# Stringing the first layer's feed-forward and the second layer's normalisation between the value and key tiles of the second layer

## The chip, the cores and the metric

The kernel runs on one core of a Trainium2 chip. The metric is the device time of one execution in microseconds (us), and the median of three runs is given. Smaller is better.

## The reference

A hidden state `x` of 16 x 64 = 1024 tokens by 512 features goes through two transformer layers, each with an attention to a fixed context `ctx` of the same shape and a feed-forward part. Each of the four parts reads a normalised `x` and adds its result to `x`:

```python
x = x + xattn0(layernorm(x), ctx, ctx, mask, Wq, Wk, Wv, Wo)       # 32 heads, 8 KV heads of 128, rope, tanh cap
x = x + lora_moe(layernorm(x), A, B, Wr)                           # 4 experts of rank 16, two chosen by a router
x = x + xattn1(layernorm(x), ctx, Wq, Wk, Wv, Wo)                  # 16 heads, 4 KV heads of 96
x = x + ffn1(layernorm(x), W, bias, A, Bf, coeffs, scales)         # dense 512x512 plus 16 weighted low-rank terms
# lora_moe: logits = x @ Wr.T; gates = softmax over the top 2;  mid = x @ A.T;  out = 4 * sum_e gates[e] * (mid[e] @ B[e].T)
# xattn1: keys and values are taken from concat(ctx, layernorm(x)); queries from layernorm(x)
```

What matters here: the feed-forward of the first layer (`lora_moe`) is small, and it stands as a chain between two attentions. Of the second attention, the keys and values of the context half depend on nothing in that chain; the queries and the keys and values of the other half do.

## The kernel before, in words

**Tiling.** The 1024 tokens are 8 tiles of 128, and the tiles 0 to 3 (`LO`) and 4 to 7 (`HI`) are normalised as two halves. Large products are made of three fp32r products (high by high, high by low, low by high: `thrice`, L1082), so each weight is split in a high part by ScalarE (ACT) and a low part by GpSimd (POOL): a `split` step. PSUM has eight banks `PB`. Banks are dealt out in turn from a list, `ring`, while banks 2 and 3 are at times reserved.

**What sets the order.** `plan()` (L63) writes out by hand one list of named steps. Every engine then walks this same list and issues what it has to do in each step, waiting on semaphores. So the list fixes the order of work on every engine at once: TensorE (PE), VectorE (DVE), ACT, POOL and the DMA queue on SyncE (SP). A blocked instruction holds up everything behind it on its engine.

**The steps that the change moves.**

- `e0(u, c)`: the first attention's output product of token tile c (12 matmuls of 512 columns); DVE adds it to `x`.
- `stats(ph, i)`, `rstd(ph, i0)`: DVE takes mean and variance of tile i, then, for four tiles at once, the reciprocal root in 12 dependent instructions. `ph` is 1 for the normalisation ahead of the feed-forward, 2 for the one ahead of the second attention.
- `xn(ph, i)` (L723): ACT writes the normalised tile into `Eb[i % 2]`; from the third tile on it waits until the tile two before it has been transposed. `xT(ph, i)`: PE transposes it (four transposes).
- `ffn_xT(i)` (L769): ACT copies the transposed tile to `pTb[i % 2]`. `mid(hf, c)`: PE multiplies it with the experts' A and the router (8 matmul instructions of 68 columns).
- `gates(hf)` (L981): on DVE, 13 steps of small dependent instructions for the router's choice of a half (a line of ACT, the exponential, in the middle), then four products that apply the gates. It waits for all four `mid` of its half.
- `mgT(hf)`: PE transposes the gated products, and ACT copies them to SBUF. `delta(i)`: PE multiplies with B (two matmul instructions of 512 columns), and DVE adds the result to `x`.
- `xsplit(2, i)`: ACT takes the high part of the transposed tile from PSUM, DVE the low part, which also frees the bank.
- `v1(w, i)` (12 matmuls of 384 columns; w = 0 is the context half, w = 1 the half from `x`), `k1(m, w, hf)` (12 matmuls of 512 columns), `q1(0, part)` (9 matmuls of 512 columns): values, keys and queries of the second attention. ACT moves each result out of PSUM. All `v1` wait for the last part of their weights, `split("wv1", 3)`; `q1(0, .)` waits for the low parts of the tiles 0 to 3 and its ACT copies for the last `delta`; `k1(., 1, 1)` waits for the low part of tile 7.

**Before the change** the order, from the last output product of the first attention on, is: `ffn_mid(0)` (L234; tiles 0 to 3: `xT`, `ffn_xT`, `mid` in turn), the gates of this half under the two context key tiles `k1(2,0,.)`, `mgT(0)`, `delta(0..3)`, `ffn_mid(1)`, two value tiles, the second normalisation of tiles 0 to 3 (`normed(2, LO)` with nothing in between), the gates of the second half, `q1(0, 0)`, `mgT(1)`, `delta(4..7)`, the rest of `q1(0, .)`, and `normed(2, HI)` with value tiles between. Then come `k1(0,1,0)`, `k1(0,1,1)` and `v1(1,0..4)`, and the loop over the 32 steps of the second attention starts; its first matmuls are those of `b1(0)` (L1257).

Of the kernel before, what the change touches and what calls it, by code (L numbers as in the profile page):

```python
# [7 lines left out]
NU = 16  # L8
N1 = 32
LO, HI = range(0, 4), range(4, 8)  # L10
# [17 lines left out]
class Plan:  # L28
# [11 lines left out]
    def step(self, *name):  # L40
        kind = name[0]
        self.at[name] = self.n[kind] = self.n.get(kind, 0) + 1
        self.steps.append(name)

    def tile(self, *name, bank=None):
        if bank is None:
            bank = self.ring.pop(0)
            self.ring.append(bank)
        self.filled[bank] += 1
        self.banks[name] = (bank, self.opened[bank], self.filled[bank])  # L50
        self.opened[bank] += 1
# [6 lines left out]
    def stage(self, *name, bank=None):  # L58
        self.tile(*name, bank=bank)
        self.step(*name)  # L60


def plan():  # L63
    p = Plan()
    step, stage, tile, ring = p.step, p.stage, p.tile, p.ring

    def split(*name):
        step("split", *name)

    def normed(ph, tiles, filler=(), first=()):  # L70
        tiles, filler = list(tiles), list(filler)
        for i in tiles[:2]:
            step("xn", ph, i)
        for f in first:
            f()
        for n, i in enumerate(tiles):
            stage("xT", ph, i)
            if n + 2 < 4:
                step("xn", ph, tiles[n + 2])
            step("xsplit", ph, i)  # L80
            f = filler.pop(0) if filler else None
            if f:
                f()
        for f in filler:
            f()
# [5 lines left out]
    def k1(m, w, hf):  # L91
        stage("k1", m, w, hf)

    def v1(w, i):
        stage("v1", w, i)
# [4 lines left out]
    def burst(u):  # L100

        if 0 <= u - 2:
            for h in range(2):
                for w in range(2):
                    tile("d0", u - 2, h, w)
                step("d0", u - 2, h)
        if 0 <= u - 1 < NU:
            stage("sum0", u - 1)
        if u < NU:
            for h in range(2):  # L110
                tile("b0", u, h, bank=2 + h)
            step("b0", u)

    def norm0(u):
        step("norm0", u)

    def e0(u, c):
        stage("e0", u, c)
# [44 lines left out]
    for u in range(NU):  # L163
# [24 lines left out]
        j, hf = u // 2 + 1, u % 2  # L188
# [11 lines left out]
        pr, m = u // 4 + 1, u % 4  # L200
# [8 lines left out]
        if u == NU - 2:  # L209
            split("wk1", 1, 0)  # L210
            split("wv1", 0)
    k1(0, 0, 1)
    burst(NU)
    k1(1, 0, 0)
    split("wv1", 1)
    e0(NU - 2, 0)
    e0(NU - 2, 1)
    norm0(NU - 1)
    split("wv1", 2)
    e0(NU - 2, 2)  # L220
    e0(NU - 2, 3)
    burst(NU + 1)
    step("ffn_load")
    k1(1, 0, 1)
    for i in LO:
        step("stats", 1, i)
    step("rstd", 1, 0)
    for c in range(4):
        e0(NU - 1, c)
        step("stats", 1, 4 + c)  # L230
    step("rstd", 1, 4)
    split("wv1", 3)

    def ffn_mid(hf, filler, first=()):  # L234
        i0, filler = 4 * hf, list(filler)
        step("xn", 1, i0)
        step("xn", 1, i0 + 1)
        for f in first:
            f()
        for c in range(4):  # L240
            stage("xT", 1, i0 + c)
            step("ffn_xT", i0 + c)
            if c + 2 < 4:
                step("xn", 1, i0 + c + 2)
            if c:
                step("mid", hf, c - 1)
            if filler:
                filler.pop(0)()
        step("mid", hf, 3)

    def ffn_gates(hf):
        p.sums("mid", hf, bank=2 + hf)
        step("gates", hf)

    def ffn_delta(hf, filler):
        stage("mgT", hf)
        for f in filler:
            f()
        for c in range(4):
            stage("delta", 4 * hf + c)  # L260

    ffn_mid(0, [])
    ffn_gates(0)
    k1(2, 0, 0)
    split("wq1", 0, 0)
    k1(2, 0, 1)
    ffn_delta(0, [])
    for i in LO:
        step("stats", 2, i)
    ffn_mid(1, [])  # L270
    step("rstd", 2, 0)
    for i in range(2):
        v1(0, i)
    for m in (1, 2):
        split("wq1", 0, m)
    ring[0:0] = [2]
    normed(2, LO)
    ffn_gates(1)
    split("wk1", 0, 1)

    def q1(g, part):
        if part < 3:
            tile("q1", g, part)
        step("q1", g, part)
        if part and g % 2 == 1 and g // 2 + 1 < 4:
            split("wq1", g // 2 + 1, part - 1)

    q1(0, 0)
    ffn_delta(1, [])
    ring[0:0] = [3]  # L290
    for i in HI:
        step("stats", 2, i)
    step("rstd", 2, 4)
    for part in range(1, 4):
        q1(0, part)
    normed(2, HI, [lambda i=i: v1(0, i) for i in range(3, 7)], [lambda: v1(0, 2)])
    v1(0, 7)
    for hf in range(2):
        k1(0, 1, hf)
    split("wk1", 1, 1)  # L300
    for i in range(5):
        v1(1, i)

    for b in (2, 3, 4, 5):
        ring.remove(b)
# [71 lines left out]
def program(nc, a, out):  # L377
# [10 lines left out]
    SC1 = 1.0 / 96.0 ** 0.5  # L388

    p = plan()  # L390
    steps, at, banks = p.steps, p.at, p.banks
    splits = {st[1:]: n for n, st in enumerate(s for s in steps if s[0] == "split")}
# [988 lines left out]
```

## Time and profile before

| | us |
|---|---|
| median of three runs | 885.11 (885.04 to 886.01) |
| the profiled execution | 885.15 |
| its span, first to last instruction | 883.4 |
| PE busy | 848.6 (96%) |
| DVE busy | 485.4 (55%) |
| ACT busy | 350.9 (40%) |
| POOL busy | 303.0 (34%) |
| mean granted TensorE clock | 0.994 of full speed |

A busy time is the sum of an engine's instructions. The span is one execution; what the profiled time has more than the span, 1.75 us, lies around the first and last instruction. In a timeline a row gives start, length, engine, line, operation, output and inputs, and in square brackets how long the engine had been idle and what released it.

### The profile page before, as it was taken

The numbers are of one execution on the slowest core, as the hardware profiler recorded it, in microseconds if no ns is written. First come the engines' busy times: TensorE is split into PE (matmuls) and PEld (weight loads), VectorE is DVE, ScalarE is ACT, GpSimd is POOL, SyncE is SP. The second block draws the span as 40 slices with busy tenths as digits, with TensorE's granted clock in tenths as the row PEclk, the third lists the DMA queues.
The fourth block names the chain that finished last, engine by engine and source line by source line (L and its number), as shares of the span: only waits on it lengthen the run. The fifth ranks groups of instructions, "written<-read, shape, count | busy, mean of one in ns | idle before, by whom it ended". The sixth has DMA issues, their size and how long they took to land.

```text
span 883.4 us, 12370 instructions
## 1 busy us (share of the span) xinstructions
PE 848.6 (96%) x4758; PEld 701.9 (79%) x4758; DVE 485.4 (55%) x876; ACT 350.9 (40%) x827; POOL 303.0 (34%) x232
## 2 busy tenths in 40 slices
PE   5999999999999999999999999979989999999998
PEld 4788887887887887877877777749978888888776
DVE  5856654755654655555565547452135544555674
ACT  5343222223123123023113233546576666766542
POOL 3386525624525525525535330010031111211132
PEclk9999999999999999999999999989999999999999
DMA  8122211311212211211212131010020110210002
GB/s 286 42 79 79 72 37 53 92 37 48 72 37 72 72 37 49 73 37 49 72 37 81 50 90 36 17 36 1 13 72 10 43 33 25 85 59 1 1 1 96
DMA packets 24891, 48.15 MB, mean 55 GB/s; under 512 B 3584, under 2 KB 4736, under 8 KB 24704
## 3 DMA queue, kind: packets, MB, share of 16 engines
q1 hardware_dynamic: 24400, 47.22, 17.9%
q8 instruction: 38, 0.62, 0.3%
q10 hardware_dynamic: 432, 0.14, 0.1%
q14 instruction: 21, 0.17, 0.1%
HBM read 45.12 MB, written 2.23 MB: 54 GB/s over the span
## 4 chain that ended last, share of the span: by engine, by line
PE 81%; ACT 9%; DVE 5%; DMA 2%; issue 2%; POOL 1%; SPq 0%; POOLq 0%; ACTq 0%; DVEq 0%
PE PB L1084 21%; PE PB L1086 20%; PE PB L1085 20%; PE PB L1242 5%; PE PB L1147 3%; PE PB L1173 2%; PE PB L1091 2%; ACT Eb L832 2%; PE PB L1257 2%; PE PB L1274 2%; DMA stage<-in_wo 2%; DVE Ol L1055 1%; ACT Oh L703 1%; PE PB L1157 1%; DVE sm L1037 1%
## 5 line engine op out<-in xcount | busy, mean ns | idle before, releaser
L662 POOL TENSOR_TENSOR qb<-qb,arena 128x512 f32<-128x512 f32 x64 | 82.6, 1291 | 128.2 <-DVE arena L942 127.8
L864 DVE TENSOR_TENSOR xs<-xs,PB 128x512 f32<-128x512 f32 x112 | 76.2, 686 | 91.7 <-PE PB L1086 84.2
L1085 PE MATMUL PB<-WOl,Oh 128*128 128x512 f32 x256 | 99.9, 390 | 0.0
L1084 PE MATMUL PB<-WOh,Oh 128*128 128x512 f32 x256 | 99.9, 390 | 0.0
L1086 PE MATMUL PB<-WOh,Ol 128*128 128x512 f32 x256 | 99.8, 390 | 0.0
L703 ACT ACTIVATE Oh<-PB 128x512 fp32r<-128x512 f32 (+2 forms) x160 | 69.1, 468 | 58.0 <-PE PB L1173 39.8
L653 POOL TENSOR_TENSOR WQl<-stage,WQh 128x512 fp32r<-128x512 f32 x38 | 48.8, 1287 | 98.9 <-ACT WQh L703 87.7
L1084 PE MATMUL PB<-xTh,WQh 128*128 128x512 f32 x192 | 77.4, 403 | 1.8 <-DVE xTl L916 1.8
L1085 PE MATMUL PB<-xTl,WQh 128*128 128x512 f32 x192 | 75.4, 393 | 0.0
L1086 PE MATMUL PB<-xTh,WQl 128*128 128x512 f32 x192 | 75.4, 393 | 0.0
L973 DVE TENSOR_TENSOR Ol<-PB,Oh 128x512 fp32r<-128x512 f32 x64 | 39.8, 684 | 64.5 <-ACT Oh L703 64.5
L939 DVE TENSOR_TENSOR qb<-PB,ropeq 128x512 f32<-128x512 f32 x64 | 44.0, 688 | 46.8 <-PE PB L1086 46.6
L653 POOL TENSOR_TENSOR WOl<-stage,WOh 128x512 fp32r<-128x512 f32 (+1 forms) x33 | 41.4, 1275 | 67.9 <-ACT WOh L703 63.9
L1055 DVE TENSOR_TENSOR Ol<-PB,Oh 96x256 fp32r<-96x256 f32 (+1 forms) x96 | 40.4, 421 | 41.6 <-ACT Oh L703 40.6
L832 ACT ACTIVATE Eb<-PB,sm 128x128 f32<-128x128 f32 x128 | 45.2, 366 | 43.5 <-DVE sm L1037 43.5
L703 ACT ACTIVATE WKh<-stage 128x512 fp32r<-128x512 f32 x12 | 7.5, 629 | 129.5 <-PE PB L1086 126.8
L1084 PEld LDWEIGHTS PB<-WOh,Oh 128*128 128x128 f32 x256 | 48.1, 188 | 10.3
L1086 PEld LDWEIGHTS PB<-WOh,Ol 128*128 128x128 f32 x256 | 48.1, 188 | 10.3
L1085 PEld LDWEIGHTS PB<-WOl,Oh 128*128 128x128 f32 x256 | 48.0, 188 | 10.2
L1091 PE MATMUL PB<-ident_sb,Eb 128*128 128x128 f32 x256 | 39.7, 281 | 11.9 <-DVE Eb L1042 5.4
L703 ACT ACTIVATE arena<-PB 128x256 f32<-128x256 f32 (+3 forms) x56 | 25.6, 470 | 64.0 <-PE PB L1086 63.6
L703 ACT ACTIVATE WQh<-stage 128x512 fp32r<-128x512 f32 x38 | 23.8, 629 | 66.6 <-PE PB L1086 66.4
(203 smaller groups left out, 2052.0 us busy)
## 6 DMA issues: line engine op xcount, KB each, us to landing
stage<-in_wq SPq DMA_DIRECT2D x44, 256.0 KB, 3.0
stage<-in_wo SPq DMA_DIRECT2D x44, 256.0 KB, 2.6
arena<-recs SPq DMA_DIRECT2D x32, 256.0 KB, 3.9
stage<-in_wk SPq DMA_DIRECT2D x14, 256.0 KB, 2.8
arena<-in_ctxT SPq DMA_DIRECT2D x8, 256.0 KB, 5.8
stage<-in_wv SPq DMA_DIRECT2D x8, 256.0 KB, 3.1
xs<-in_x SPq DMA_DIRECT2D x8, 256.0 KB, 6.3
out<-xs SPq DMA_DIRECT2D x8, 256.0 KB, 2.0
```

The lines of the kernel that those rows point to most:

```text
L653: e.tensor_tensor(lo, staged[:, n % 4, 0:cols], hi.bitcast(f32), ALU.subtract).then_inc(s_wlo)
L662: e.tensor_tensor(dst, dst, tmp, ALU.add).then_inc(s_radd)
L703: return e.activation(dst, src, ACT.Copy)
L832: last = e.activation(Eb[:, e2, cols], PS[:, cols], ACT.Exp, bias=mx[:, bb:bb + 1], accum_out=rs[:, bb:bb + 1])
L864: e.tensor_tensor(xs[:, i, :], xs[:, i, :], PB[b][:, :], ALU.add).then_inc(free[b])
L939: e.tensor_tensor(dst, src, table[:, 0:1, :].broadcast_to([128, 8, 64]), ALU.mult)
L1055: last = e.tensor_tensor(dl, src, dh.bitcast(f32), ALU.subtract)
L1084: e.matmul(dst, Ah, Bh, start=(k == 0), stop=False)
L1085: e.matmul(dst, Ah, Bl, start=False, stop=False)
L1086: return e.matmul(dst, Al, Bh, start=False, stop=(k == n - 1))
L1091: last = e.transpose(dst[:, c * 128:(c + 1) * 128], src[:, c * 128:(c + 1) * 128], ident[:, :])
L1242: last = e.matmul(PB[b][:, :], W[:, m, r], H[:, c, cols], start=(n % 12 == 0), stop=(n % 12 == 11))
```

## The change

The list of steps is rewritten between the first attention's last products and the loop of the second attention. No instruction is added or taken away; the helpers `ffn_mid`, `ffn_gates` and `ffn_delta` give way to single steps in a new order. In short:

- `stats(1, i)` of the tiles 0 to 3 follow each `e0(14, i)`, and `rstd(1, 0)` stands ahead of the `e0(15, .)`, so `xn`, `xT` and `ffn_xT` of tiles 0 and 1 stand between the last `e0`.
- The `mid` come in pairs. `k1(2,0,0)` stands between the `mid` of tiles 1 and the `xT` of tile 2; `k1(2,0,1)` stands behind `gates(0)` and the second pair of `mid`; `split("wv1", 3)` now stands behind `gates(0)`.
- `v1(0,0)` stands ahead of `mgT(0)`. The transposes and `mid` of tiles 4 and 5 and the transposes of 6 and 7 come before `delta(0..3)`; `v1(0,1)` and the last two `mid` after. Each `delta(i)` has its `stats(2, i)` right behind it.
- `v1(0,2..5)` stand around `rstd(2,0)` and `gates(1)`; `v1(0,6)` and `v1(0,7)` and `mgT(1)` stand between the transposes of the second normalisation of tiles 0 to 3. Then `delta(4..7)`, all four parts of `q1(0, .)`.
- The second normalisation of tiles 4 to 7 is strung with `k1(0,1,0)` and `v1(1,0..2)`, followed by `v1(1,3)`, `k1(0,1,1)` and `v1(1,4)`.

```diff
--- before.py
+++ after.py
@@ -209,74 +209,23 @@
         if u == NU - 2:
             split("wk1", 1, 0)
             split("wv1", 0)
-    k1(0, 0, 1)
-    burst(NU)
-    k1(1, 0, 0)
-    split("wv1", 1)
-    e0(NU - 2, 0)
-    e0(NU - 2, 1)
-    norm0(NU - 1)
-    split("wv1", 2)
-    e0(NU - 2, 2)
-    e0(NU - 2, 3)
-    burst(NU + 1)
-    step("ffn_load")
-    k1(1, 0, 1)
-    for i in LO:
-        step("stats", 1, i)
-    step("rstd", 1, 0)
-    for c in range(4):
-        e0(NU - 1, c)
-        step("stats", 1, 4 + c)
-    step("rstd", 1, 4)
-    split("wv1", 3)
-
-    def ffn_mid(hf, filler, first=()):
-        i0, filler = 4 * hf, list(filler)
-        step("xn", 1, i0)
-        step("xn", 1, i0 + 1)
-        for f in first:
-            f()
-        for c in range(4):
-            stage("xT", 1, i0 + c)
-            step("ffn_xT", i0 + c)
-            if c + 2 < 4:
-                step("xn", 1, i0 + c + 2)
-            if c:
-                step("mid", hf, c - 1)
-            if filler:
-                filler.pop(0)()
-        step("mid", hf, 3)
-
-    def ffn_gates(hf):
+    def stats(ph, i):
+        step("stats", ph, i)
+
+    def ffn_xT(i):
+        stage("xT", 1, i)
+        step("ffn_xT", i)
+
+    def mid(i):
+        step("mid", i // 4, i % 4)
+
+    def gates(hf):
         p.sums("mid", hf, bank=2 + hf)
         step("gates", hf)
 
-    def ffn_delta(hf, filler):
-        stage("mgT", hf)
-        for f in filler:
-            f()
-        for c in range(4):
-            stage("delta", 4 * hf + c)
-
-    ffn_mid(0, [])
-    ffn_gates(0)
-    k1(2, 0, 0)
-    split("wq1", 0, 0)
-    k1(2, 0, 1)
-    ffn_delta(0, [])
-    for i in LO:
-        step("stats", 2, i)
-    ffn_mid(1, [])
-    step("rstd", 2, 0)
-    for i in range(2):
-        v1(0, i)
-    for m in (1, 2):
-        split("wq1", 0, m)
-    ring[0:0] = [2]
-    normed(2, LO)
-    ffn_gates(1)
-    split("wk1", 0, 1)
+    def delta(i):
+        stage("delta", i)
+        stats(2, i)
 
     def q1(g, part):
         if part < 3:
@@ -285,21 +234,89 @@
         if part and g % 2 == 1 and g // 2 + 1 < 4:
             split("wq1", g // 2 + 1, part - 1)
 
-    q1(0, 0)
-    ffn_delta(1, [])
+    k1(0, 0, 1)
+    burst(NU)
+    k1(1, 0, 0)
+    split("wv1", 1)
+    for c in range(4):
+        e0(NU - 2, c)
+        stats(1, c)
+        if c == 1:
+            norm0(NU - 1)
+            split("wv1", 2)
+    burst(NU + 1)
+    step("ffn_load")
+    k1(1, 0, 1)
+
+    step("rstd", 1, 0)
+    for c in range(4):
+        e0(NU - 1, c)
+        stats(1, 4 + c)
+        if c < 2:
+            step("xn", 1, c)
+        else:
+            ffn_xT(c - 2)
+            step("xn", 1, c)
+    for i in range(2):
+        mid(i)
+    k1(2, 0, 0)
+    for i in (2, 3):
+        ffn_xT(i)
+    step("rstd", 1, 4)
+    for i in (4, 5):
+        step("xn", 1, i)
+    gates(0)
+    for i in (2, 3):
+        mid(i)
+    split("wv1", 3)
+    k1(2, 0, 1)
+    split("wq1", 0, 0)
+    for i in (4, 5):
+        ffn_xT(i)
+        step("xn", 1, i + 2)
+    v1(0, 0)
+    stage("mgT", 0)
+    for i in (4, 5):
+        mid(i)
+    for i in (6, 7):
+        ffn_xT(i)
+    for i in LO:
+        delta(i)
+    v1(0, 1)
+    for i in (6, 7):
+        mid(i)
+    for m in (1, 2):
+        split("wq1", 0, m)
+    step("rstd", 2, 0)
+    for i in range(2, 5):
+        v1(0, i)
+    for i in range(2):
+        step("xn", 2, i)
+    gates(1)
+    v1(0, 5)
+    ring[0:0] = [2]
+    for i in range(4):
+        stage("xT", 2, i)
+        if i < 2:
+            step("xn", 2, i + 2)
+        step("xsplit", 2, i)
+        if i < 2:
+            v1(0, 6 + i)
+        if i == 1:
+            split("wk1", 0, 1)
+        if i == 2:
+            stage("mgT", 1)
+    for i in HI:
+        delta(i)
     ring[0:0] = [3]
-    for i in HI:
-        step("stats", 2, i)
     step("rstd", 2, 4)
-    for part in range(1, 4):
+    for part in range(4):
         q1(0, part)
-    normed(2, HI, [lambda i=i: v1(0, i) for i in range(3, 7)], [lambda: v1(0, 2)])
-    v1(0, 7)
-    for hf in range(2):
-        k1(0, 1, hf)
+    normed(2, HI, [lambda i=i: v1(1, i) for i in range(3)], [lambda: k1(0, 1, 0)])
+    v1(1, 3)
+    k1(0, 1, 1)
     split("wk1", 1, 1)
-    for i in range(5):
-        v1(1, i)
+    v1(1, 4)
 
     for b in (2, 3, 4, 5):
         ring.remove(b)
```

## Rows read from the trace of the kernel before

**Rows 1.** The page: busy time by engine; then shares of the chain that ended last.

```profile
PE 848.6 (96%) x4758; PEld 701.9 (79%) x4758; DVE 485.4 (55%) x876; ACT 350.9 (40%) x827; POOL 303.0 (34%) x232
...
PE 81%; ACT 9%; DVE 5%; DMA 2%; issue 2%; POOL 1%; SPq 0%; POOLq 0%; ACTq 0%; DVEq 0%
```

**Rows 2.** Busy time by stretch: PE, PEld, DVE, ACT, POOL, granted clock, DMA share, GB/s.

```profile
561.00:563.00 2.00, 0.73 (x5) 0.35 (x3) 0.00 (x0) 1.42 (x3) 1.01 (x1) 1.00 0.00 0
579.00:587.00 8.00, 6.12 (x20) 4.41 (x21) 5.47 (x17) 4.36 (x8) 1.36 (x2) 0.57 0.22 66
```

**Rows 3.** Timeline of PE, 548 to 630 us, from the last `e0` to the loop.

```profile
548.12 0.39 PE L1086 MATMUL PB<-W,Ol 128*128 128x512 f32 x1
...
549.89 1.42 PE L1091 MATMUL PB<-ident_sb,Eb 128*128 128x128 f32 x8 [1.38 <-ACT Eb L728]
...
563.20 1.99 PE L1208 MATMUL PB<-qb 64*128 64x512 f32 x8 [1.47 <-ACT qb L703]
...
578.26 1.36 PE L1091 MATMUL PB<-ident_sb,Eb 128*128 128x128 f32 x8 [2.95 <-ACT Eb L728]
...
583.66 0.80 PE L1242 MATMUL PB<-xTh,WQh 128*128 128x512 f32 x1 [1.41 <-DVE xTl L916]
...
589.34 1.99 PE L1208 MATMUL PB<-qb 64*128 64x512 f32 x8 [0.56 <-ACT qb L703]
...
630.07 1.05 PE L1257 MATMUL PB<-arena,qb 96*128 96x128 f32 x8
```

**Rows 4.** Timeline of PE, same stretch: row starts give the length of each step.

```profile
552.18 0.60 PE L1091 MATMUL PB<-ident_sb,Eb 128*128 128x128 f32 x4
...
552.62 1.01 PE L1194 MATMUL PB<-qb,pTb 128*128 128x68 f32 x8
...
555.67 0.47 PE L1084 MATMUL PB<-cTh,WQh 128*128 128x512 f32 x1
...
561.35 0.38 PE L1091 MATMUL PB<-ident_sb,qb 128*128 128x128 f32 x2
...
591.26 0.50 PE L1242 MATMUL PB<-xTh,WQh 128*128 128x512 f32 x1
...
597.55 0.34 PE L1084 MATMUL PB<-WVh,cTh 128*128 128x384 f32 x1
...
617.56 0.33 PE L1084 MATMUL PB<-WVh,xTh 128*128 128x384 f32 x1
```

**Rows 5.** Timeline of ACT, 550 to 604 us.

```profile
550.58 0.60 ACT L703 ACTIVATE pTb<-PB 128x512 f32<-128x512 f32 x1
...
557.77 0.21 ACT L782 ACTIVATE qb<-qb 128x16 f32<-128x16 f32 x1 [3.07 <-DVE qb L1007]
...
561.54 1.19 ACT L703 ACTIVATE arena<-PB 96x512 f32<-96x512 f32 x2 [0.94 <-PE PB L1086]
...
598.98 1.52 ACT L728 ACTIVATE Eb<-xs,lnb 128x512 f32<-128x512 f32 x2
...
600.52 0.98 ACT L703 ACTIVATE V<-PB 64x384 f32<-64x384 f32 x2
...
602.86 0.97 ACT L703 ACTIVATE V<-PB 64x384 f32<-64x384 f32 x2
```

**Rows 6.** Timeline of DVE, 555 to 587 us.

```profile
555.90 0.17 DVE L993 COPY qb<-PB 128x16 f32<-128x16 f32 x1 [3.33 <-PE PB L1194]
...
564.43 2.48 DVE L864 TENSOR_TENSOR xs<-xs,PB 128x512 f32<-128x512 f32 x4 [4.96 <-PE PB L1208]
...
572.33 0.16 DVE L909 SCALAR_TENSOR_TENSOR lnb<-mv,lnb 128x4 f32<-128x4 f32 x1
...
586.26 1.30 DVE L1016 SCALAR_TENSOR_TENSOR qb<-qb 128x16 f32<-128x16 f32 x1
```

**Rows 7.** Timeline of POOL, low parts of weights.

```profile
549.26 1.00 POOL L653 TENSOR_TENSOR WOl<-stage,WOh 128x384 fp32r<-128x384 f32 x1 [23.75 <-ACT WOh L703]
...
586.25 1.28 POOL L653 TENSOR_TENSOR WKl<-stage,WKh 128x512 fp32r<-128x512 f32 x1 [6.64 <-issue]
```

## The prediction, made before the changed kernel was run

> **What bounds the kernel now.** Read the page first: PE is busy for 96% of the span and holds 81% of the chain that ended last [rows 1]. Nothing that DVE, ACT or POOL do counts unless PE waits for it, and a new order of steps can win only time in which PE waits or runs slowly. So the next view is PE's timeline, from the last `e0` matmul to the first matmul of the loop, `b1(0)` [rows 3]. An "idle before" there understates a loss: matmul ends are modelled, and a step that trickles shows no gap. I therefore compare elapsed time with work. A last matmul holds PE for one spacing, (597.55 - 591.26) / 27 = 0.233 us, so the stretch begins at 548.12 + 0.23 = 548.35 and lasts to 630.07: 81.7 us [rows 3, 4].
>
> Work in it, each length a difference of starts [rows 3, 4]: four transposes 552.62 - 552.18 = 0.44; a `mid` (555.67 - 552.18 - 0.88) / 3 = 0.87; a `k1` (561.35 - 555.67) / 2 = 2.84; `mgT`, two transposes, 0.22; four `delta` 591.26 - 589.34 = 1.92; a `v1` (630.07 - 617.56) / 6 = 2.085; 36 `q1` matmuls 36 x 0.233 = 8.4. Sum: 16 tiles of transposes 7.0, 8 `mid` 7.0, 4 `k1` 11.4, 2 `mgT` 0.4, 8 `delta` 3.8, 14 `v1` 29.2, `q1` 8.4 = 67.2. So 81.7 - 67.2 = 14.5 us are lost before the loop. By place [rows 3, 4]: 1.5 before 549.89 (for the first `xn`), 0.6 up to 552.18, 1.6 before 563.20 (561.35 to 563.20 less 0.22: first gates and `mgT` copy), 3.7 between 563.20 and 578.26 (two value tiles are all that stands under statistics, weight splits and `xn`), 3.6 between 578.26 and 583.66 (5.40 for 1.76 of transposes), 3.3 up to 589.34 (5.68 for nine `q1` matmuls, 2.1, and `mgT`). The stretches 552.18 to 561.35 and from 597.55 on lose nothing beyond rounding. A part of this is clock: from 579 to 587 the granted clock averages 0.57, which is mostly the 1.2 GHz level, after the long wait that ended at 578.26; elsewhere, as at 561 to 563 with PE busy for 0.73 of 2.00 us, it stays at 1.00, 2.4 GHz [rows 2].
>
> **The change part by part.** All instructions and all DMAs stay. The order of `split` steps, and with it SP's order of loads, is the same; each load waits for the low part four splits earlier. `split("wv1", 3)` and those behind it come later against PE, the tightest case is below. I walk the new list on the old clock, with these hand-overs: a PE step's end to ACT or DVE 0.2 us, ACT or DVE to PE 0.06 (550.58 + 0.60 is followed by a `mid` at once) [rows 5].
>
> 1. *Ahead of the last `e0`.* `stats(1,0..3)` and `rstd(1,0)` go into DVE idle time; they cost nothing there as long as the normalised E0 product of step 15, which waits for a DMA, and the `Ol` parts are not pushed back. `xn(1,0)` is then ready before 541, so the 1.5 us before 549.89 go. The transposes of tile 0 start at 545.6, ahead of `e0(15,3)`, those of tile 1 at 548.8; `ffn_xT(1)` ends at 548.8 + 0.7 + 0.6 = 550.1, `mid(0)` fills the time but for 0.05.
> 2. *First wait that stays.* `mid(1)` ends at 551.0, `k1(2,0,0)` at 553.8, the transposes of tiles 2 and 3 at 554.7. On ACT the eviction of `k1(2,0,0)`, 1.2 us [rows 5], stands ahead of `ffn_xT(2)`: 554.0 to 555.2, copy to 555.8. PE waits from 554.7 to 555.9: **1.2 us**.
> 3. *First gates.* Two `mid` end at 557.6. DVE starts 0.23 later, the exponential 557.77 - 555.90 = 1.87 after that, at 559.7 [rows 5, 6]; `split("wv1", 3)` is behind it: 559.8 on ACT, POOL from 560.4 for 1.00 us [rows 7]. `v1(0,0)` can start at 561.5. PE has `k1(2,0,1)` and two tiles of transposes until 561.3: **0.2 us**. The gates' second half meets this POOL instruction on DVE. Before, the L1016 instruction at 586.26 took 1.30 us beside a POOL instruction of 1.28 [rows 6, 7]; at most 1.1 us is added, so the gated products are ready by 562.5, while `mgT(0)` comes at 563.6.
> 4. *Deltas.* `mgT(0)` 563.6, two `mid`, two tiles of transposes to 566.4. Its ACT copy stands behind `xn(1,7)` and the eviction of `v1(0,0)` and ends at 566.3. Both arrive together: 0 to 0.3 us. The banks which the deltas take were freed at 563 to 566.3.
> 5. *Second normalisation, tiles 0 to 3.* Before, DVE went from the first `delta` sum to the end of `rstd` in 572.33 + 0.16 - 564.43 = 8.1 us [rows 6]. Now that is 567.0 to 575 or 576; PE has `v1(0,1)`, two `mid` and `v1(0,2..4)` until 578.3, so it is hidden with 2 us to spare, and would cost its excess beyond that. What is late next is ACT's own queue. From the eviction of `v1(0,4)` at 578.5: 1.0; two `xn` 1.5; exponential of `gates(1)` 0.2; eviction, `xn`, high part twice over, each 602.86 - 600.52 = 2.34; eviction 1.0; `wk1` split 0.6 (taken as the 512-column copy of 550.58); high part 0.5; `mgT(1)` copy 0.4, both set somewhat under that copy. Sum 9.9, so it ends near 588.5 [rows 5]. PE has `v1(0,5..7)`, four transposed tiles and `mgT(1)`: 6.3 + 1.8 + 0.2 from 578.3, to 586.6. **2.0 us** of wait, then the deltas.
> 6. *Last part.* Deltas and `q1(0, .)` take 10.3 us, and DVE needs 8.1 for sums, statistics and `rstd(2,4)`: hidden. Then ACT has 2.34 us per string of eviction, `xn` and high part, PE 2.085 + 0.44 = 2.53. It keeps up; `k1(0,1,1)` needs the low part of tile 7, some 0.1 us before its turn because `v1(1,3)` stands ahead.
>
> Sum: 67.2 of work, 1.2 + 0.2 + 2.0 and 0.1 for the small ones: 70.7 instead of 81.7, a gain of 11.0 us. Changing between kinds of matmul may cost up to 0.1 each at some eight new places (a first `q1` matmul after deltas takes 0.50 against the 0.39 of 548.12 [rows 3, 4]); I take it as nothing and keep 0.8 as the bound. The clock dip is in the 11.0, as its cause, the 3 us wait, goes. The loop is entered 11 us sooner with ACT and DVE caught up; its own waits stay. The profiled 885.15 becomes 874.1; it stands 0.04 above the median, so the forecast is 874.1 for both.
>
> **The rivals.**
>
> *A clock dip returns* (chance 0.12). The 2.0 us wait is followed by four `delta` of 64 rows, then by `q1`. Before, 7 to 8 us went at the low level after a wait of about 3 us [rows 2, 3]. In full matmuls that costs half of it, 3.5 us: 877.6. Against it: waits of 1.5 and 1.6 us, the latter before the same deltas, left the clock at 1.00.
>
> *Each link of the strings waits a little* (0.12). ACT is in order, so every `xn` or high part stands behind an eviction that waits for PE. Before, with nothing between, four tiles took 5.40 instead of 1.76 (0.9 each). If the eight tiles of step 5 and 6 lose half of that each, 3.6: 877.7; with all of it, 881.
>
> *The gain comes back in the loop* (0.02). If ACT, loads or splits set the time at which the loop runs, b1(0) comes earlier and the time stays at 885. PE's 81% of the chain speaks against it [rows 1].
>
> *Slower than before: the low clock stays for the whole chain* (0.04). Many short stops replace three long ones: pairs of `mid`, single tiles of transposes and 64-row deltas with waits of 0.2 to 2.0 us between. If PE stays at the lower level from the `xT` of tile 1 (549) to the first `q1` (590.5), 41 us, 20.5 more are needed, less 3.4 of waits that such a PE no longer meets: 874.1 + 17 = 891. It decides from 22 us at the low level on, where it eats the 11. Against it: the same mixture ran at 1.00 before, with more waiting in it [rows 2].
>
> That rival has a page behind it. The Trainium skill, "TensorE: Matmul & The Clock Gate", section "A second HAM failure mode: psum-queue depth-cycling", says that short idle moments between groups of matmuls, while PSUM banks are cycled, can make the clock swing between its two levels. By this rule the time would be that rival's; by the row of 561 to 563 it is the forecast. The trace sides against the rule here, since the clock held through such stops.
>
> **How the numbers follow.** The forecast has 0.70. Its own range: the wait of step 5 may be 1 to 3, that of step 2 0.5 to 1.8, switches 0 to 0.8, small extras 0 to 1, and some of the work may overlap better by 0.5: 872.5 to 876.5. The two rivals near 877.6 are taken in: 872.0 to 878.5 leaves out 0.04 + 0.02 and the outer part of the links, with a rest for errors of the walk, 0.2 in all. Within 0.2% (1.8 us), what a measurement of this kernel can tell from no change, lies only the third rival. Faster 0.94, same 0.02, slower 0.04.
>
> **What would show it.** PE's timeline after: `xT(1,0)` directly behind `e0(15,2)`; a wait of about 1.2 us before the `mid` of tile 2, released by ACT's `pTb`; about 2 us before `delta(4)`, released by ACT's `qb` copy; no wait over 0.5 us elsewhere up to `b1(0)`, which starts near 619; granted clock 1.00 from 40 us on. It is wrong if the clock row shows a dip, if the strings of normalisation show a wait at each tile, or if `b1(0)` comes at 619 and the end does not follow.

## The result, and the profile after

| | before | after |
|---|---|---|
| median, us | 885.48 (885.04 to 886.01, 4 runs) | 874.52 (873.64 to 875.48, 4 runs) |
| profiled execution and its span | 885.15, 883.4 | 875.48, 873.7 |
| mean granted clock of the profiled execution | 0.994 | 0.996 |

The ratio is 0.9878, with a 95% interval of 0.9866 to 0.9890. The forecast was 874.1 us, for the median and for the profiled execution alike: the median came out 0.4 us above it, the profiled execution 1.4. (A fourth run moved the median of the kernel before from 885.11 to 885.48.) The change was run twice more beside experiments, on two chips: 873.76 (5 runs; ratio 0.9868, 0.9850 to 0.9886) and 873.71 (5 runs; 0.9873, 0.9854 to 0.9893). One execution of 3000 us, the profiled one among the five of that last median, and one of 1224 us of the kernel before are far slower than all others, and the ratios leave them out.

Busy times and shares hardly change; the lines that answer to [rows 1]:

```profile
PE 846.7 (97%) x4758; PEld 701.8 (80%) x4758; DVE 487.3 (56%) x876; ACT 351.7 (40%) x827; POOL 303.3 (35%) x232
...
PE 82%; ACT 9%; DVE 4%; DMA 2%; issue 1%; POOL 1%; SPq 0%; POOLq 0%; ACTq 0%; DVEq 0%
```

PE's timeline after, from the first transposes of the feed-forward to the loop. It answers to [rows 3, 4].

```profile
546.47 0.60 PE L1108 MATMUL PB<-ident_sb,Eb 128*128 128x128 f32 x4
...
549.66 0.60 PE L1108 MATMUL PB<-ident_sb,Eb 128*128 128x128 f32 x4
...
550.10 1.96 PE L1211 MATMUL PB<-qb,pTb 128*128 128x68 f32 x16
...
551.86 0.48 PE L1101 MATMUL PB<-cTh,WQh 128*128 128x512 f32 x1
...
554.75 1.04 PE L1108 MATMUL PB<-ident_sb,Eb 128*128 128x128 f32 x8
...
556.82 2.00 PE L1211 MATMUL PB<-qb,pTb 128*128 128x68 f32 x16 [1.03 <-ACT pTb L720]
...
561.51 1.03 PE L1108 MATMUL PB<-ident_sb,Eb 128*128 128x128 f32 x8
...
562.64 0.42 PE L1101 MATMUL PB<-WVh,cTh 128*128 128x384 f32 x1
...
567.75 1.99 PE L1225 MATMUL PB<-qb 64*128 64x512 f32 x8
...
587.72 0.60 PE L1108 MATMUL PB<-ident_sb,Eb 128*128 128x128 f32 x4
...
590.10 1.99 PE L1225 MATMUL PB<-qb 64*128 64x512 f32 x8 [1.78 <-ACT qb L720]
...
592.01 0.50 PE L1259 MATMUL PB<-xTh,WQh 128*128 128x512 f32 x1
...
620.33 1.05 PE L1274 MATMUL PB<-arena,qb 96*128 96x128 f32 x8
```

The reader is to see three things. The transposes of tile 0 (546.47) stand ahead of `e0(15,3)`, and those of tile 1 (549.66) right behind it, where the kernel before still waited for the first normalised tile. There are two waits, 1.03 us released by the `pTb` copy and 1.78 us by the `mgT(1)` copy (by starts 556.82 - 554.75 - 0.88 = 1.19 and 590.10 - 587.72 - 0.44 = 1.94). And the four deltas of the second half take 592.01 - 590.10 = 1.91 us, as before, thus at full speed.

What ends the second wait is ACT's queue: eviction of `v1(0,7)`, the `wk1` split and one high part ahead of the copy at 589.57.

```profile
587.43 0.97 ACT L720 ACTIVATE V<-PB 64x384 f32<-64x384 f32 x2
...
588.43 0.63 ACT L720 ACTIVATE WKh<-stage 128x512 fp32r<-128x512 f32 x1
...
589.08 0.60 ACT L720 ACTIVATE xTh<-PB 128x512 fp32r<-128x512 f32 x1
...
589.57 0.38 ACT L720 ACTIVATE qb<-PB 128x256 f32<-128x256 f32 x1
```

The granted clock (third number from the end) after the start is 1.00 throughout, and around both waits too; it answers to [rows 2]. In this profile the lower level is left at the start of the kernel alone.

```profile
22.00:30.00 8.00, 6.54 (x17) 5.21 (x18) 5.01 (x12) 3.73 (x9) 1.28 (x1) 0.57 0.29 89
554.00:558.00 4.00, 2.97 (x23) 2.50 (x22) 0.00 (x0) 3.02 (x6) 0.00 (x0) 1.00 0.00 0
588.00:592.00 4.00, 2.22 (x11) 0.85 (x9) 2.33 (x4) 2.39 (x5) 1.27 (x1) 1.00 0.06 14
40.00:873.00 833.00, 816.16 (x4621) 676.90 (x4619) 460.77 (x808) 335.90 (x799) 289.97 (x214) 1.00 0.17 49
```

Where did the time go? From the start of `e0(15,3)`, 545.63, to `b1(0)`, 630.07, the kernel before takes 84.44 us. The same work now runs from 546.47 (the transposes that precede `e0(15,3)`) to 620.33: 73.86 us, so 10.6 us less. From `b1(0)` to the end of the span it is 253.3 in both. Up to 546, the profiled execution after is 0.84 us later than before. At the start of the kernel its clock averaged 0.57 from 22 to 30 us, against 0.79 in the kernel before. That differs from execution to execution: the second profile of the changed kernel has 0.79 there too, and reaches the same place at 544.78.

### The profile page after: what moved, and what is told of

It is laid out like the page before. It is cut to its first block, busy times and chain, and to the rows that moved or that the text cites. A ratio compares the mean times of both kernels' runs of the same rounds, so it can differ in the third digit from the quotient of the medians.

```text
span 873.7 us, 12372 instructions
## 1 busy us (share of the span) xinstructions
PE 846.7 (97%) x4758; PEld 701.8 (80%) x4758; DVE 487.3 (56%) x876; ACT 351.7 (40%) x827; POOL 303.3 (35%) x232
## 4 chain that ended last, share of the span: by engine, by line
PE 82%; ACT 9%; DVE 4%; DMA 2%; issue 1%; POOL 1%; SPq 0%; POOLq 0%; ACTq 0%; DVEq 0%
PE PB L1101 21%; PE PB L1103 21%; PE PB L1102 21%; PE PB L1259 5%; PE PB L1164 3%; PE PB L1190 2%; ACT Eb L849 2%; PE PB L1108 2%; PE PB L1274 2%; PE PB L1291 2%; DMA stage<-in_wo 2%; DVE Ol L1072 1%; ACT Oh L720 1%; PE PB L1174 1%; DVE sm L1054 1%
## 5 line engine op out<-in xcount | busy, mean ns | idle before, releaser
L1101 PEld LDWEIGHTS PB<-xTh,WQh 128*128 128x128 f32 x192 | 36.7, 191 | 14.9 <-issue 7.6
```

The costliest lines, as they stand in the source:

```text
L1101: e.matmul(dst, Ah, Bh, start=(k == 0), stop=False)
```

## The experiments

"The stretch" is from `e0(15,3)`, or the transposes right ahead of it, to `b1(0)`: 84.44 us before, 73.86 after (73.84 in the second profile of the changed kernel, 544.78 to 618.62). The stretches of the experiments come from one profile each. All ratios are to the kernel before on the same chip; differences from the changed kernel are across chips where the text doesn't say otherwise.

**1. Only the head of the change** (`e2_head`).

```diff
-    e0(NU - 2, 0)
-    e0(NU - 2, 1)
...
+    for c in range(4):
+        e0(NU - 2, c)
+        step("stats", 1, c)
...
+        if c < 2:
+            step("xn", 1, c)
+        else:
+            stage("xT", 1, c - 2)
+            step("ffn_xT", c - 2)
+            step("xn", 1, c)
```

> The kernel before with the head of the change alone: stats(1,i) behind each e0(14,i), rstd(1,0) ahead of e0(15,.), xn of tiles 0 and 1 and xT(1,0), xT(1,1) between the last e0; from the mid of tile 0 on the order is the old one. Theory, that lost time adds up by place: the 1.5 us before the first transposes and 0.5 in the first group go, all else shifts with them, 2.0 us faster than before (1.6 to 2.4). Rival: the time saved reappears at the next wait, for the first gates, because that is bound by ACT or DVE: 0 to 0.5 us faster.

Measured: 884.45 us, ratio 0.9987 (0.9976 to 0.9999), 1.0 us less than before and half of what was expected; the stretch is 83.84 us (544.69 to 628.53), 0.6 less. PE's timeline of it:

```profile
560.17 1.99 PE L1217 MATMUL PB<-qb 64*128 64x512 f32 x8 [1.47 <-ACT qb L712]
...
575.23 2.67 PE L1100 MATMUL PB<-ident_sb,Eb 128*128 128x128 f32 x12 [2.95 <-ACT Eb L737]
...
580.64 0.50 PE L1251 MATMUL PB<-xTh,WQh 128*128 128x512 f32 x1 [1.41 <-DVE xTl L925]
...
585.32 0.41 PE L1100 MATMUL PB<-ident_sb,qb 128*128 128x128 f32 x2 [2.34 <-DVE qb L1029]
...
586.30 3.51 PE L1217 MATMUL PB<-qb 64*128 64x512 f32 x7 [0.56 <-ACT qb L712]
...
589.76 0.50 PE L1251 MATMUL PB<-xTh,WQh 128*128 128x512 f32 x1
...
628.53 1.05 PE L1266 MATMUL PB<-arena,qb 96*128 96x128 f32 x8
```

`delta(0)` starts 15.48 us after the stretch's start, against 17.57 before: the 2.1 us are there. They are still there at the second `mgT` (585.32 - 544.69 = 40.63, against 588.36 - 545.63 = 42.73) and at `delta(4)` (41.61 against 43.71). In between, `q1(0,0)` ran at full speed and PE then waited 2.34 us for the second gates instead of 0.94, which cancels out: the gates came 2.1 us sooner like all else. So the rival, that the time saved comes back at a wait for the gates, did not happen. What is lost is lost in the four deltas of the second half, which take 589.76 - 586.30 = 3.46 us instead of 1.92, and that is the clock:

```profile
586.00:590.00 4.00, 3.70 (x9) 1.51 (x10) 1.37 (x3) 0.15 (x1) 0.00 (x0) 0.57 0.12 47
```

**2. The clock alone, first try** (`e1_clock`).

```diff
                     pe.wait_ge(s_ident, 16)
+                    if ph == 2 and i == 0:
+                        for _ in range(24):
+                            turn(PB[b], ident, 1)
                     pe.wait_ge(*xn_done(ph, i))
```

> The kernel before, with 24 transposes of the constant matrix put on PE ahead of its wait for xn(2,0), into the bank that xT(2,0) then overwrites: they fill about 2.6 of the 3.1 us wait that ended at 578.26. Nothing else changes. It asks how much of the gain of the change is the granted clock and how much is waits. My theory: the clock stays at 1.00 from 575 to 592, q1(0,0) (nine matmuls) shrinks from 3.6 to 2.1 us, but the time hardly moves, since the gates of the second half on DVE, which stand behind the four low parts, set when mgT(1) can go; only the last transposes being faster brings these 0.5 us forward. So 0.3 to 1.0 us faster than before. Rival, the clock as the cause: 7.2 us at the lower level give back half of it, 3.5 us faster. Third: the clock falls all the same, and nothing moves.

Measured: 887.12 us (883.25 to 891.88, 12 runs), ratio 1.0015 (0.9998 to 1.0032). It is none of the three as stated, and nearest to the third. The clock held where PE was kept busy (576 to 588), yet in the profiled execution, one of the two longest of the twelve, it fell twice elsewhere, once behind a wait of only 1.38 us and once behind one of 1.75:

```profile
548.68 1.43 PE L1091 MATMUL PB<-ident_sb,Eb 128*128 128x128 f32 x8 [1.38 <-ACT Eb L728]
...
587.11 0.50 PE L1245 MATMUL PB<-xTh,WQh 128*128 128x512 f32 x1 [1.75 <-DVE xTl L916]
```
```profile
546.00:550.00 4.00, 2.48 (x14) 1.59 (x12) 2.61 (x10) 2.56 (x5) 1.01 (x1) 1.00 0.00 0
550.00:562.00 12.00, 12.00 (x53) 11.17 (x53) 4.08 (x24) 3.27 (x6) 0.00 (x0) 0.57 0.08 23
576.00:588.00 12.00, 9.00 (x61) 7.64 (x60) 3.48 (x10) 8.08 (x14) 2.50 (x2) 1.00 0.15 44
588.00:600.00 12.00, 10.10 (x28) 5.63 (x27) 7.46 (x22) 2.31 (x5) 1.27 (x1) 0.57 0.08 22
```

The stretch took 91.86 us (544.42 to 636.28), 7.4 more than in the profile of the kernel before. So in the old order the low level can strike at several places. The first of the two falls came ahead of the edit. The 12 runs line up with their granted clock: 883.25 and 884.56 at 0.998, 891.41 at 0.988 and 891.88 at 0.990. The 59 executions of the kernel before that were timed beside the experiments do the same: median 883.9 at 0.996 (10 runs), 885.0 at 0.994 (24), 885.3 at 0.992 (12), 887.3 at 0.990 (10), 889.0 at 0.988 (3).

**3. The clock held through the whole stretch, waits untouched** (`e9_fill`). `fill` is n transposes of the constant matrix into the bank that the step then overwrites.

```diff
+                    fill(PB[b], {(1, 0): 12, (2, 0): 24, (2, 3): 1}.get((ph, i), 0))
                     pe.wait_ge(*xn_done(ph, i))
...
+                    fill(PB[b], 8 * hf)
                     pe.wait_ge(*read("mid", hf))
...
+                    fill(PB[b], {0: 12, 4: 4}.get(i, 0))
                     pe.wait_ge(*read("mgT", hf))
...
+                    if (g, part) == (0, 0):
+                        pe.wait_ge(*opened("q1", 0, 0))
+                        fill(PB[bank_of("q1", 0, 0)], 11)
```

> The kernel before, with each of its larger waits in the stretch filled with transposes of the constant matrix on PE (12 before the transposes of tile 0, 12 and 4 before delta(0) and delta(4), 24 and 1 before those of tiles 0 and 3 of the second normalisation, 11 before q1(0,0), 8 before mgT(1)): the waits stay as long, but PE is never still for more than a few tenths of a us. It separates waits from clock, which e1_clock could not, since there the clock fell elsewhere in the stretch. Theory: the clock stays at 1.00 from 40 us on in every execution; as ACT's and DVE's chains end the waits, the time falls only to the lower edge of the kernel before, 883 to 884 us (1 to 2 us), and the wider spread of the kernel before goes. Rival, clock as the main cause of the 11 us: 879 or less.

Measured: 884.34 us (882.16 to 885.14, 12 runs; the kernel before 884.12 to 889.03), ratio 0.9979 (0.9966 to 0.9992): 0.7 to 3.0 us faster than before, and with a narrower spread, as the theory said. The stretch is 84.15 us (545.78 to 629.93), of which 545 to 600 is all at 1.00:

```profile
545.00:600.00 55.00, 51.23 (x320) 42.34 (x319) 30.19 (x106) 28.00 (x49) 6.05 (x5) 1.00 0.08 25
```
```profile
578.44 1.36 PE L1096 MATMUL PB<-ident_sb,Eb 128*128 128x128 f32 x8 [0.34 <-ACT Eb L728]
...
583.74 0.50 PE L1253 MATMUL PB<-xTh,WQh 128*128 128x512 f32 x1 [0.55 <-DVE xTl L916]
...
588.32 0.43 PE L1096 MATMUL PB<-ident_sb,qb 128*128 128x128 f32 x2 [1.36 <-DVE qb L1020]
...
589.23 1.99 PE L1216 MATMUL PB<-qb 64*128 64x512 f32 x8
...
629.93 1.05 PE L1268 MATMUL PB<-arena,qb 96*128 96x128 f32 x8
```

With full speed through the stretch, the chain on ACT and DVE brings `q1(0,0)` and `mgT(1)` within 0.2 us of where they were (583.66 in [rows 3] and 588.36, now 583.74 and 588.32). So of the 10.6 us that the change takes off the stretch, 10.3 (84.15 - 73.86) are waits and 0.3 is clock in the profiled executions. Over many executions the clock weighs more: 0.9 us by the medians (884.34 against 885.24), 1.9 by the ratio. The longest executions of the old order, at mean clocks down to 0.988, suggest more than one fall in each, but none of them was profiled save that of `e1_clock`.

**4. The second normalisation not strung** (`e6_bare`).

```diff
-    v1(0, 5)
+    for i in (5, 6, 7):
+        v1(0, i)
...
-        if i < 2:
-            v1(0, 6 + i)
```

> The changed kernel, with the second normalisation of tiles 0 to 3 not strung: v1(0,6) and v1(0,7) stand ahead of its four transposes instead of between them. Theory, walking ACT's queue: after the eviction of v1(0,7) it has two xn, high parts, the wk1 split, and the mgT(1) copy in a row, which ends 1.35 us later than now; the wait before delta(4) is the only one that grows, and the time is 1.3 us over the changed kernel (1.0 to 1.8), some 9.7 under before. Rival: bare transposes cost what they cost before, 0.9 us a tile, 3.6 us over the changed kernel.

Measured: 876.83 us, 3.1 over the changed kernel on its second run (873.76) and 2.3 over its first; the stretch is 76.52 us (545.13 to 621.65), 2.66 over. The waits are 1.13 + 0.47 + 1.14 us in place of 1.78, so 0.96 more, and the deltas take 593.34 - 590.00 = 3.3 us instead of 1.9. The walk was right on the total of the waits to 0.4 us, but not on their place: the one before `delta(4)` did not grow, and two new ones came before the transposes. And it left out the clock, whose average from 588 to 594 is 0.72. The rival's 3.6 us is nearer in number, but its waits before the transposes are 1.6 us, and the slower deltas add 1.4.

```profile
586.91 0.63 PE L1107 MATMUL PB<-ident_sb,Eb 128*128 128x128 f32 x4 [1.13 <-ACT Eb L744]
...
588.24 0.63 PE L1107 MATMUL PB<-ident_sb,Eb 128*128 128x128 f32 x4 [0.47 <-ACT Eb L744]
...
590.00 3.40 PE L1224 MATMUL PB<-qb 64*128 64x512 f32 x8 [1.14 <-ACT qb L719]
```
```profile
588.00:594.00 6.00, 4.62 (x15) 2.27 (x16) 3.97 (x8) 2.35 (x6) 1.27 (x1) 0.72 0.17 46
```

**5. A longer wait, and the same wait filled** (`e7_wait3`, `e10_wait3fill`).

```diff
                     act.wait_ge(*done("mgT", hf))
+                    for n in range(13 if hf else 0):
+                        move(qb[:, 0, 1536 + 16 * n:1552 + 16 * n], PB[b][:, 0:16])
```

and for the second also `fill(PB[b], 22)` ahead of `delta(4)`'s wait.

> The changed kernel, with 13 copies of 16 columns on ACT ahead of the copy of mgT(1), about 1.6 us: the wait before delta(4) grows from 1.8 to about 3.4 us. It measures the rival of a clock dip. If a wait of this length brings the lower level, as the 3.1 us wait did before, the four deltas and part of q1 run at it, and the time is 3 to 5 us over the changed kernel; if the clock holds, exactly the added 1.6 us.

> e7_wait3 with 22 transposes of the constant matrix on PE in its 2.7 us wait before delta(4). The wait stays, PE is not still. Theory: in e7_wait3 the longer wait cost 0.9 us itself and 1.6 us by the four deltas running at the lower level; with the fill the deltas take 1.9 instead of 3.5 us and the time is 1.6 us under e7_wait3, 875.4 us. Rival: the copies on ACT slow something else, and the fill changes nothing: 877 us.

Measured: 877.13 us (876.60 to 877.35, 4 runs) without the fill, 875.70 us (874.89 to 876.56, 5 runs, another chip) with it; the stretches are 76.39 us (545.76 to 622.15) and 74.75 (544.94 to 619.69). PE without the fill, then with it:

```profile
590.35 2.93 PE L1227 MATMUL PB<-qb 64*128 64x512 f32 x6 [2.71 <-ACT qb L720]
...
593.82 0.50 PE L1261 MATMUL PB<-xTh,WQh 128*128 128x512 f32 x1
```
```profile
590.00:594.00 4.00, 3.65 (x9) 1.46 (x10) 2.12 (x4) 0.70 (x2) 0.00 (x0) 0.57 0.20 70
```

```profile
589.45 1.99 PE L1233 MATMUL PB<-qb 64*128 64x512 f32 x8 [0.26 <-ACT qb L720]
```
```profile
586.00:594.00 8.00, 7.74 (x49) 5.81 (x48) 5.25 (x10) 3.83 (x19) 1.28 (x1) 1.00 0.13 35
```

The 13 small copies cost 0.9 us and not 1.6 (with the `mgT` copy, 14 took 1.37). The wait grew from 1.94 to 2.86 us by starts, and this was enough: the deltas took 593.82 - 590.35 = 3.47 us. With PE kept busy they took 1.9. The same wait at the two levels differs by 1.64 us in the stretch, 1.4 in the medians. So the first rival of the prediction is real: it stayed away behind a wait of 1.94 us and came behind one of 2.86, and here its price is 1.6 us, not 3.5.

**6. Better orders** (`e3_mid2`, `e4_delta4`, `e5_both`; the changed kernel beside them, `a1_after`).

```diff
+    for i in (2, 3):
+        ffn_xT(i)
     k1(2, 0, 0)
-    for i in (2, 3):
-        ffn_xT(i)
```

```diff
+        if i == 2:
+            stage("mgT", 1)
         step("xsplit", 2, i)
-        if i < 2:
-            v1(0, 6 + i)
-        if i == 1:
-            split("wk1", 0, 1)
-        if i == 2:
-            stage("mgT", 1)
+        if i in (0, 2):
+            v1(0, 6 + i // 2)
+    split("wk1", 0, 1)
```

> The changed kernel itself once more, beside the three below, so that they can be compared on one chip: 10.5 to 11.5 us under before.

> The changed kernel with the transposes and copies of tiles 2 and 3 ahead of k1(2,0,0) instead of behind it, so that ACT copies them before it evicts the key tile. Theory: the 1.0 us wait before the mid of tile 2 (1.2 by starts) goes, the first gates come as much sooner, nothing else moves: 1.2 us under the changed kernel. Rival: xn(1,3) or the gates become the bound and half or more of it comes back before v1(0,0): 0 to 0.6 us.

> The changed kernel with the steps of the second normalisation of tiles 0 to 3 in another order: mgT(1) and its ACT copy ahead of the high part of tile 2, v1(0,7) behind them, the wk1 split last. Theory: the wait of 1.9 us before delta(4) is ACT's queue (eviction, split and high part ahead of the copy), so it goes; a new one of 0.35 us comes before q1(0,0), whose tile 3 is now split 1 us later. 1.5 us under the changed kernel (1.2 to 1.9). Rival: the gates on DVE set the wait, not ACT's queue, and nothing moves.

> Both edits of e3_mid2 and e4_delta4. Theory, that waits on PE add up: 2.7 us under the changed kernel, near 871.5 us. Rival: not additive, 1.5 to 2.0.

| | median, us | ratio (95%) | stretch, us | against 73.86 |
|---|---|---|---|---|
| `a1_after` | 873.71 | 0.9873 (0.9854 to 0.9893) | not measured | |
| `e3_mid2` | 873.06 | 0.9862 (0.9844 to 0.9879) | 72.42 | -1.44 |
| `e4_delta4` | 872.91 | 0.9859 (0.9837 to 0.9881) | 72.40 | -1.46 |
| `e5_both` | 871.72 | 0.9845 (0.9826 to 0.9864) | 70.96 | -2.90 |

In the stretch all three come out within 0.25 us of the walk (1.2, 1.5 and 2.7), and they add up. The medians move less (0.7, 0.8, 2.0 us), and e4_delta4 spreads from 870.49 at clock 1.000 to 875.05 at 0.996, so single edits of 1 us are not told apart by medians of four to six. What is left in e5_both is one wait of 0.3 us, as expected, and 70.7 of 71 us with PE busy:

```profile
587.69 0.50 PE L1258 MATMUL PB<-xTh,WQh 128*128 128x512 f32 x1 [0.29 <-DVE xTl L932]
```
```profile
545.00:616.00 71.00, 70.71 (x413) 62.94 (x412) 33.88 (x108) 44.52 (x80) 7.41 (x6) 1.00 0.07 20
```

**7. The start** (`e11_start`): e5_both with `fill(PB[b], 10)` before the fourth tile of the first normalisation and `fill(PB[b], 14)` before `q0(0,0)`.

> e5_both with PE's two waits at the start of the kernel filled with transposes of the constant matrix: 10 in the wait before the fourth tile of the first normalisation and 14 in the wait of 1.75 us before q0(0,0). In the profiles of the changed kernel and of e5_both the lower level held from 22 or 23 to 26 to 29 us, behind these waits, where q0 matmuls took 0.43 us each. Theory: the clock then stays at 1.00 over the whole execution, and the time settles at the best executions of e5_both, 870.2 us, with a spread under 1 us. Rival: the level falls all the same, since the transposes are too little work, and the median stays at 871.7.

Measured: 870.09 us (869.87 to 871.37, 5 runs), ratio 0.9825 (0.9796 to 0.9853); every execution has a granted clock of 1.000. The median is as expected, and the spread of 1.5 us is wider than the 1 us expected. This is the fastest version: 1.75% under the kernel before and 3.6 us under the changed one (873.71, same chip, timed earlier). That it is faster than `e5_both` (871.72; 870.17 to 872.46, same chip) rests on four and five executions whose ranges overlap; all at 1.000 against a clock down to 0.996 is the clearer sign.

```profile
20.00:30.00 10.00, 9.26 (x57) 8.24 (x58) 8.04 (x16) 5.70 (x13) 3.36 (x4) 1.00 0.27 81
40.00:868.00 828.00, 813.85 (x4605) 675.13 (x4603) 458.67 (x806) 333.29 (x797) 288.67 (x214) 1.00 0.17 49
```

> The changed kernel once more, on the same chip as the two above: 873.5 to 874.5 us, 11 us under before; if any execution is above 875, its granted clock is lower than that of the others.

That last run gave 873.76; its five executions are 873.28 at 1.000 to 874.29 at 0.998, and none is above 875.

## Why the prediction was right

**Work and losses.** It took 67.2 us of work, plus 2.7 for `e0(15,3)`, and 3.5 of waits: 73.4 for the stretch. Measured: 73.86, with 3.6 of waits (1.19 + 0.25 + 0.10 + 1.94 + 0.14) and 70.2 of work. The 0.3 between is about what switches between kinds of matmul would take, which had been put at 0 to 0.8; it was not measured by itself.

**Step 1** held: no wait is left ahead of the first `mid`. Experiment 1 shows its 2.1 us alone, kept up to `delta(4)`.

**Step 2** held: 1.2 predicted, 1.19 measured, released by ACT as named; experiment 6 removes it by taking the copy from behind the eviction.

**Step 3** held, in detail too. The exponential came 1.87 us after the first gate instruction (560.73 and 558.86), the wait before `v1(0,0)` was 562.64 - 561.51 - 0.88 = 0.25 for 0.2, and the instruction beside POOL's low part took 0.92 us. In the second gates, with POOL idle, it took 0.17, so that is 0.75 more, of at most 1.1 allowed:

```profile
561.61 0.92 DVE L1033 SCALAR_TENSOR_TENSOR qb<-qb 128x16 f32<-128x16 f32 x1
```
```profile
561.49 1.00 POOL L670 TENSOR_TENSOR WOl<-stage,WOh 128x384 fp32r<-128x384 f32 x1 [35.11 <-ACT WOh L720]
```

Both end at 562.5. The Trainium skill, "SBUF — State Buffer", section "Who interferes with whom", has a rule that fits: a VectorE instruction with two SBUF inputs and a GpSimd one that reads SBUF share one read interface, and the later one waits. The trace agrees, here and in [rows 6, 7]; as forecast, nothing hangs on it.

**Step 4**: 0.10 us within 0 to 0.3. **Step 5** held: 9.9 us of ACT's queue were added up, and the copy ended 589.95 - 580.08 = 9.9 us after the eviction of `v1(0,4)` began; wait 1.94 for 2.0. That ACT's order and not the gates sets it is shown by e4_delta4. **Step 6** held: from 592.01 on PE never waits over 0.14 us.

**The clock.** Of the time lost before the loop the prediction said that "a part of this is clock", without a size. Experiment 3 gives the part: 0.3 us of the stretch. The low level fell on transposes and on nine `q1` matmuls, and the gates behind them set when PE went on anyway. But the prediction read one execution as the kernel. Others of the old order meet more of the low level, and the change takes that away as well, which the sum did not have.

**Luck.** The mechanism held, and the last few tenths are luck. The stretch gave 10.6 us where the sum had 11.0, and between the two profiled executions the start took 0.84 back, so they differ by 9.7. The medians differ by 11.0, 11.3 and 11.5 in the three comparisons: the 0.4 to 0.9 above the stretch is of the size of the clock's share in experiment 3. That this second term makes up for what the sum had too much was not foreseen. The range "of its own", 872.5 to 876.5, is also narrower than its terms: added straight, the bounds give 871.9 and 877.5.

**The rivals.** The clock dip did not happen in either profile of the changed kernel, but it stood closer than its 0.12 suggests: about one more us of waiting brings it, in one wait (experiment 5) or in three short ones (experiment 4). Its price was set too high for this place, since the level came back within 4 us and struck four deltas alone; the profile of experiment 2, with two longer falls, is 7.4 us longer in the stretch than that of the kernel before. The links of the strings cost 0.14 us at most. The slower side did not come. The Trainium skill's rule of short idle moments ("TensorE: Matmul & The Clock Gate", section "A second HAM failure mode: psum-queue depth-cycling") was dismissed in the prediction with one window of the old order at 1.00. That was too quick: the profile of `e1_clock` shows the old order falling behind a 1.38 us wait among short matmuls, and that of `e6_bare` a fall behind waits of 1.13, 0.47 and 1.14 us, so there the trace agrees with the rule. For the changed order itself no profile shows a fall in the stretch.

**Open.** No experiment edits alone what fills the 3.7 us before the second normalisation (value tiles over statistics and `rstd`) or the strings of tiles 4 to 7; their part rests on the timelines and on the sum. Why the clock fell behind waits of 1.4 and 1.75 us in one execution and held behind 1.94 in others stays open. Why two executions of the changed kernel took 875.0 and 875.7 us at a clock of 0.998 was not seen, since neither was profiled.

## What to carry to other kernels

When one engine is busy nearly all the time and steps are only moved, add up the work of the stretch from differences of starts, subtract it from the elapsed time, and walk the in-order queue of each helper engine: that gave 11.0 us for 10.6 measured. The waits that stay are found by the same walk, and stand where a copy that PE needs is queued behind an eviction that nobody needs yet. Read the granted clock of many executions, not of one. And count several short waits close together like a long one: here both brought the lower level, and filling the wait kept it away.

## What the runs showed of the hardware

- A granted clock of 0.57 over 590 to 594 us came behind a wait of 2.9 us (e7_wait3), none behind one of 1.9 (changed kernel, two profiles). The length of the last wait alone does not decide it. Behind a wait of 1.4 us among short matmuls the clock fell in one profile (e1_clock) and not in another (kernel before); it also fell behind one of 1.75 us (e1_clock), behind three waits of 1.13, 0.47 and 1.14 us (e6_bare), and behind waits of 2.34 and 0.56 us with only two transposes between them (e2_head).
- Four deltas (8 matmul instructions) took 1.9 us at the full level and 3.3 to 3.5 us behind a fall (e6_bare, e2_head and e7_wait3).
- Transposes of a constant during a wait kept the clock at 1.00 over that wait in all four profiles where they were tried (e1_clock, e9_fill, e10_wait3fill, e11_start), with no cost that shows: 875.70 instead of 877.13 us, and 870.09 instead of 871.72. With a single wait filled, the clock fell at others (e1_clock).
- The same program differs by up to 6 us between executions, mostly in step with the clock: 883.0 to 889.3 us in 59 executions of the kernel before, at mean clocks of 0.996 and 0.988.
